# Gated delta rule and feed-forward kernel: the lower parts of the weights made by TensorE and ScalarE instead of VectorE

## What is computed

```python
xn = layernorm(x)
static = xn @ W.T
k = rmsnorm(xn by head, 16 heads of 8) * k_norm_w
o = scan(k, static, lam, beta)             # the gated delta rule: S = lam*S; S += beta*k (v - k^T S); o = k^T S
x = x + layernorm(static + o)
      + ffn(xn)
# ffn: h = silu(xn @ w1.T * s1) * (xn @ w2.T * s2)
#      h = gelu(h @ h1.T * t1); h = gelu(h @ h2.T * t2); out = h @ w3.T * s3
# all of w1, w2 (512x128), h1, h2 (512x512) and w3 (128x512) hold only -1, 0 and 1
```

## Time and profile before

| | us |
|---|---|
| median of 3 executions | 791.06 (790.12 to 791.97) |
| the profiled execution | 785.81 |
| its span, first to last instruction | 784.1 |
| of that, `prepare`, to the first instruction of the second part | 142.1 |
| clock of TensorE granted over the span | 0.985 of full |

### The profile page before, as it was taken

The page is one execution under the profiler, slowest core; times in us unless marked ns, Lnnn a source line. Parts: engine busy times, 40 slices in busy tenths (PEclk is TensorE's granted clock), DMA queues, the critical chain, the costliest instruction groups (busy, mean ns, idle before and its releaser), DMA issues.

```text
span 784.1 us, 13111 instructions
## 1 busy us (share of the span) xinstructions
PE 712.4 (91%) x3349; PEld 513.9 (66%) x3349; DVE 726.6 (93%) x2036; ACT 587.3 (75%) x1363; POOL 645.4 (82%) x640
## 2 busy tenths in 40 slices
PE   4888886599999999999999999777699999999998
PEld 3434343478888888888888888643356666666655
DVE  5999999899999999999999999996789898899987
ACT  6888886689898888889988898764665556657631
POOL 3787889797888979979898898767799789989873
PEclk9999999899999999999999999997999999999999
DMA  5677865501613325171161241501622212120001
GB/s 128 207 261 247 274 223 202 144 15 30 133 40 81 81 61 113 41 147 41 42 146 41 59 89 56 156 26 34 187 82 82 68 41 68 54 70 27 1 27 41
DMA packets 139241, 75.75 MB, mean 97 GB/s; under 512 B 74922, under 2 KB 123052, under 8 KB 139180
## 3 DMA queue, kind: packets, MB, share of 16 engines
q1 hardware_dynamic: 138124, 74.58, 34.4%
q10 hardware_dynamic: 1056, 0.52, 0.2%
HBM read 39.86 MB, written 33.55 MB: 94 GB/s over the span
## 4 chain that ended last, share of the span: by engine, by line
DVE 47%; PE 27%; issue 3%; ACT 2%; POOL 2%; DVEq 0%; POOLq 0%; ACTq 0%; SPq 0%
DVE r_rec L1271 11%; DVE r_gain L1283 9%; DVE r_pg L1257 9%; DVE r_kw L1277 9%; PE f_ps L2429 7%; PE f_ps L2430 6%; DVE r_rec L1291 6%; PE f_ps L2406 5%; DVE l_qs L1345 2%; PE r_rec L2464 1%; PE r_rec L2458 1%; PE r_rec L2448 1%; PE f_ps L2437 1%; PE r_rec L2446 1%; PE f_ps L2397 1%
## 5 line engine op out<-in xcount | busy, mean ns | idle before, releaser
L1672 POOL TENSOR_TENSOR l_kv<-l_qkv 128x1024 f32<-128x1024 f32 x64 | 124.5, 1950 | 18.3 <-PE f_ps L2430 16.6
L1271 DVE TENSOR_REDUCE r_rec<-r_pg 128x32 f32<-128x288 f32 x256 | 129.3, 505 | 0.6 <-ACT r_pg L1891 0.6
L1283 DVE TENSOR_REDUCE r_gain<-r_kw 128x64 f32<-128x256 f32 x256 | 118.7, 464 | 0.0
L1345 DVE TENSOR_TENSOR l_qs<-f_ps,l_qd 128x1024 f32<-128x1024 f32 x64 | 78.1, 1221 | 26.7 <-PE f_ps L2430 19.7
L1542 POOL TENSOR_TENSOR f_hl<-f_h,f_hh 128x512 fp32r<-128x512 f32 x64 | 80.9, 1298 | 24.7 <-ACT f_hh L1937 24.3
L2293 PE MATMUL f_ps<-f_gh,w_hi 128*128 128x512 f32 x256 | 100.0, 391 | 0.9 <-POOL f_gl L1542 0.7
L2293 PE MATMUL f_ps<-f_hh,w_hi 128*128 128x512 f32 x256 | 99.8, 390 | 0.0
L1550 POOL TENSOR_TENSOR f_g<-f_a,f_b 128x512 f32<-128x512 f32 x64 | 82.3, 1297 | 16.3 <-ACT f_b L1926 16.1
L1291 DVE SCALAR_TENSOR_TENSOR r_rec<-r_rec,lam,r_gain 128x64 f32<-128x64 f32 x256 | 86.6, 338 | 0.4 <-ACT r_w L1902 0.3
L1542 POOL TENSOR_TENSOR f_gl<-f_g,f_gh 128x512 fp32r<-128x512 f32 x64 | 82.6, 1304 | 0.0
L1352 DVE TENSOR_REDUCE l_o_in<-l_qs 128x128 f32<-128x1024 f32 x64 | 77.2, 1211 | 0.5
(11 more groups left out here) (229 smaller groups left out, 2088.1 us busy)
## 6 DMA issues: line engine op xcount, KB each, us to landing
scratch_xnT<-p_xnT SPq DMA_DIRECT2D x16, 256.0 KB, 2.9
scratch_K<-p_kout SPq DMA_DIRECT2D x16, 256.0 KB, 2.3
scratch_fac<-p_fac SPq DMA_DIRECT2D x16, 256.0 KB, 2.3
scratch_R<-p_rr SPq DMA_DIRECT2D x16, 256.0 KB, 2.3
scratch_P<-p_pp SPq DMA_DIRECT2D x16, 256.0 KB, 3.0
first_x<-scratch_xnT SPq DMA_DIRECT2D x16, 256.0 KB, 3.6
first_xt<-in_L_attn_x_dram SPq DMA_DIRECT2D x16, 256.0 KB, 2.9
scratch_W<-r_w SPq DMA_DIRECT2D x16, 256.0 KB, 4.2
```

Source lines behind the costliest of these rows:

```text
L1271: dve.tensor_reduce(w_here(g, blk), pg[q][:, at, :, :, :].rearrange("p (v g) i k -> p v g i k", g=G)[:, :, g, :, :], AX.X, ALU.add).then_i ...
L1283: dve.tensor_reduce(of_group(g, gain), of_group(g, kw), AX.X, ALU.add).then_inc(gain_ok, 1)
L1672: pool.tensor_tensor(dst, k, v, ALU.mult).then_inc(kv_ok, 1)
```

## The change

VectorE loses `lower`. TensorE gets one: with `minus`, a new 128 x 128 tile that holds minus the identity as fp32r and is written once by GpSimd, it multiplies the four squares of `w_hi` (512 columns) and adds the product onto the turned weights that still lie in `ps_f` (`start=False`), so that the bank holds `ps_f - w_hi`. It stands in step k between `static` and `couplings` and waits for `hi_done`. ScalarE gets a `lower` that copies the bank to `w_lo`; it stands between `root_mean` and `factors` and waits for the product. The semaphore `tr_done` now counts twice for each group. Nothing else moves.

```diff
--- before.py
+++ after.py
@@ -198,6 +198,7 @@
         nath = sb("nath", [P, 2, NB, HID])
         nat3, nat_ws = sb("nat3", [P, HID]), sb("nat_ws", [P, P])
         par, work = sb("par", [P, 3]), sb("work", [P, 16])
+        minus = sb("minus", [P, P], F32R)
         ones, o_bias, o_hi, s3 = sb("ones", [P, P]), sb("o_bias", [P, P]), sb("o_hi", [2 * ROW, P], F32R), sb("s3", [P, P])
         dec_t = sb("dec_t", [P, L])
         peak, ftmp = sb("peak", [P, PEAKS]), sb("ftmp", [1, 2])
@@ -425,6 +426,7 @@
                 pool.affine_select(out=heads, in_=heads, compare_op=ALU.is_ge, fill=0.0,
                                    base=0, pattern=[[-DH, H], [0, DH]], channel_multiplier=1).then_inc(pool_chain, 1)
                 pool.wait_ge(const_done, 1)
+                pool.tensor_scalar(minus[:, :], c.ident[:, :], -1.0, None, ALU.mult)
                 pool.tensor_copy(c.by_place[:, :].rearrange("p (s i b) -> p s i b", i=BLK, b=BSEG),
                                  c.ident[:, :].rearrange("p (s b i) -> p s i b", i=BLK, b=BSEG)).then_inc(const_done, 1)
                 pool.wait_ge(pool_chain, 5)
@@ -529,8 +531,12 @@
                     act.activation(fac[n.slot][:, :], ps_f[:, :, :].rearrange("p a b -> p (a b)"), ACT.Identity,
                                    scale=c.gate[:, :], bias=1.0).then_inc(fac_ok, 1)
 
+                def lower(g):
+                    act.wait_ge(tr_done, 2 * g + 2)
+                    act.activation(c.w_lo[:, NB * g:NB * g + NB, :], ps_f[:, :, :], ACT.Copy).then_inc(lo_done, 1)
+
                 def upper(g):
-                    act.wait_ge(tr_done, g + 1)
+                    act.wait_ge(tr_done, 2 * g + 1)
                     act.activation(c.w_hi[:, NB * g:NB * g + NB, :], ps_f[:, :, :], ACT.Copy).then_inc(hi_done, 1)
 
                 def exponentials():
@@ -578,6 +584,8 @@
                     at(of(k - 1), normed)
                     at(of(k - 2), static)
                     at(of(k - 1), root_mean)
+                    if 0 <= k - 3 < NG - 1:
+                        lower(k - 3)
                     at(of(k - 3), factors)
                     if k == B + 1:
                         key_squares(of(B - 1))
@@ -659,13 +667,8 @@
                 dve.sem_inc(ssq_ok, 1)
                 dve.sem_inc(prod_ok, 2)
                 dve.sem_inc(r_step, 2 * SWEEPS)
-                def lower(g):
-                    dve.wait_ge(hi_done, g + 1)
-                    dve.tensor_tensor(c.w_lo[:, NB * g:NB * g + NB, :], ps_f[:, :, :], c.w_hi[:, NB * g:NB * g + NB, :].bitcast(F32),
-                                      ALU.subtract).then_inc(lo_done, 1)
-
                 def last_weight():
-                    dve.wait_ge(tr_done, NG)
+                    dve.wait_ge(tr_done, 2 * NG - 1)
                     dve.wait_ge(scales_in, SCALES)
                     dve.tensor_tensor(c.w3[:, :, :], ps_f[:, :, :], s3[:, :].unsqueeze(1).to_broadcast([P, NB, P]),
                                       ALU.mult).then_inc(w3_done, 1)
@@ -726,9 +729,7 @@
                 for k in range(B + 3):
                     at(of(k), statistics)
                     at(of(k), aggregate)
-                    if 0 <= k - 3 < NG - 1:
-                        lower(k - 3)
-                    elif k - 3 == NG - 1:
+                    if k - 3 == NG - 1:
                         last_weight()
                     at(of(k - 1), square_sums)
                     at(of(k - 3), solve, 0)
@@ -804,6 +805,13 @@
                     for _ in range(n):
                         nc.tensor.matmul(ps_n[:, 0, 0:P], c.head_ones[:, :], c.ident[:, :], start=True, stop=True)
 
+                def lower(g):
+
+                    pe.wait_ge(hi_done, g + 1)
+                    nc.tensor.matmul(ps_f[:, :, :].rearrange("p a b -> p (a b)"), minus[:, :],
+                                     c.w_hi[:, NB * g:NB * g + NB, :].rearrange("p n d -> p (n d)"),
+                                     start=False, stop=True, skip_group_check=True).then_inc(tr_done, 1)
+
                 pe.wait_ge(const_done, 4)
                 pe.wait_ge(ws_in, 16)
                 nc.tensor.transpose(ps_s[:, 0, :], nat_ws[:, :], c.ident[:, :]).then_inc(ws_tr, 1)
```

## The result

The changed kernel takes 1098.28 us (median of four, 1096.4 to 1099.5) against 791.51 us for the kernel before: ratio 1.388, 95% interval [1.385, 1.391], 307 us slower. The forecast was 809.8 us with a range of 805 to 825: wrong. What came is the rival that the forecast had given a chance of 0.03 ("about 1,100 in all"), and on top of it a part of the one with 0.08, the clock.

A forecast was written before the change was run, and what follows sets the result against it. VectorE sets the pace, a ScalarE-TensorE ring only 0.14 us shorter. Nine steps going from 7.65 to 9.65 us add 17.7, step 3 adds 2.0, less 0.2 and 0.8: 791.06 + 18.7 = 809.8 us, range 805 to 825.

The forecast's parts named there:

- the clock: Rival, preparation steps: longer TensorE pause ahead of `factors` drops the clock to 1.2 GHz; 831 to 852 us, chance 0.08.
- The change doesn't do what it says: Rival: lower parts in the bank not zero, flag set, second part runs 1280 more products; about 1,100 us, chance 0.03.
- The price of the flag: Second part, if the flag is set: 1280 more products at 0.23 us each, up to 294 us.
- The ring: Chain through ScalarE and TensorE, one couplings copy to the next, preparation steps 3 to 12: 9.65 us a changed step.
- The round trip: ScalarE idle between its lower copy and its `factors`, waiting for TensorE's `factors` product: 1.34 us a step.
- The copy: ScalarE's copy of the bank to `w_lo`, directly ahead of `factors`, ten steps: 0.57 us each.
- The product: TensorE's added product between `static` and `couplings`, ten steps: 0.23 us each, 0.39 as the other end.
- Slack of the old ring: Before the change, the chain through ScalarE and TensorE was put about 0.14 us shorter than VectorE's 7.65 us step.
- VectorE's gain: VectorE's subtraction removed, 0.66 us in each of ten steps: worth nothing, since VectorE then waits for ScalarE.
- The 0.8 us back after step 12: From step 13 VectorE, rested, starts its first solve sooner after the couplings' copy: 0.8 us less.

## Why the prediction was wrong, point by point

- **The flag.** The failing step is the paragraph "The change doesn't do what it says". It named the rule, the mechanism and the time (1,100 us; measured 1098) and gave them 0.03. The forecast took it that a product with `start=False` adds to all that the four transposes have left; in the runs it left zero in the last square of each group and values over 0.5 in the third, and the flag came on. No row of the trace spoke for that; the page spoke against it; and the kernel's own `attended` (L2448) sets each such product directly behind its own transpose, which is a form that the rule allows. The kernel before even holds the form that was missing: `straight` fills a bank in four parts with `start=t == 0` (L2458), and `final` then adds to all four without a start (L2464). A source with a definite rule, and nothing against it, should have made this the likeliest case, or at least have put its time in the range.
- **The price of the flag.** Up to 294 us by 1280 x 0.23; measured 285.4 between the profiles, 0.223 us a product. Right.
- **The ring.** Forecast 9.65 us a step; at full clock 9.51. The round trip was put at 1.34 us: ScalarE's idle time ahead of `factors` is 1.23 us. The copy 0.57: 0.62. The product 0.23: 0.24. Slack of the old ring 0.14: 0.20 (7.45). VectorE's gain worth nothing: shown, by a run that takes only VectorE's subtraction away. The terms were right within 0.15 us.
- **The clock.** The rival had a chance of 0.08 and 831 to 852 us. It came in a mild form: 0.8 us a step and not 4.2, since only part of each step ran at 1.2 GHz. With the flag held off, the couplings of step 12 came at 127.0 us instead of 99.1, + 27.9 us; ten steps at full clock would have given about 19 (10 x 1.86). The chance leaned on one stretch with an unbroken clock. Its longest pause was 1.86 us (first line, of before). With the change, the first step with a pause of 2.26 us was slow already; the next one had the full clock, and all behind it up to step 12 were slow (second line, step 3 with the flag held off, columns as in rows 2):

```profile
18.30 2.02 PE L771 MATMUL p_ps_s<-p_xnT,ws_t 128*128 128x512 f32 x2 [1.86 <-ACT p_xnT L499]
```

```profile
24.50:34.15 9.65, 7.11 (x18) 3.97 (x19) 6.06 (x22) 5.33 (x13) 5.46 (x8) 0.65 0.49 163
```

The length of one pause isn't all of it: the version without the lower part has steps at 0.83 with pauses of 1.53 us.

- **The 0.8 us back after step 12** didn't show: from the couplings of step 12 to the second part it took 43.8 us (127.02 to 170.80) against 43.0 before (99.09 to 142.1). The clock in that stretch was 0.92; it wasn't tried apart.
- With the flag off the forecast of 809.8 would have been 5 us short of 814.7, inside its range. In differences it is 18.7 against 25.2 us; the unread products in the pause gave some 8.7 us of that back (ratio 1.020 against 1.031), which more than covers the missing 6.5, so the clock is the missing part.

## What to carry to other kernels

Ask of a matmul that adds onto what others left in a bank which of them started the bank last: a start for each part of a bank is harmless while nobody adds, but a later product with `start=False` over all parts doesn't add to all of them: here it added to the last and not to the third. Where a flag guards an expensive branch, a change to the data behind the flag is to be costed at the branch's price too.

An engine at 95% can be relieved for nothing. Follow one step around before believing the share, and, of a moved instruction, look at what waits for it: in front of the instruction that needs its result by way of another engine it cost 1.8 us a step at full clock (9.51 against 7.69), and in a wait that was there anyway nothing.

## What the runs showed of the hardware

- Four fp32 transposes in one bank, each with its own start, and then one product over all 512 columns without one: in the last 128 columns the sum is right (zero), and in the third 128 values over 0.5 stand in its place. With one start, at the first, the sums are zero in all, in ten groups out of ten.
- With a pause of 2.26 us in every step, TensorE's granted clock was 0.83 in most steps (10.3 us each), though TensorE was busy two thirds of a step at full clock (6.38 of 9.51 us). With 0.94 us of unread products in the pause it was 1.00 in nearly all steps and 0.94 over 60 us.
- Two kernels whose preparation differs by 27 us have second parts of 927.40 and 927.40 us. With the flag off the second part took 642.0 to 644.6 us in the ten profiles: a part behind a common barrier can be compared alone, to some 3 us.
